# Experts' results computed and stored in quarters of the groups instead of halves, with batch 1's results read last, in a two-layer gated cross-attention kernel

## The reference, cut to what matters

```python
grouped = x.reshape(b, s // g, g, d)                      # g = 32 tokens to a group, 128 groups in all
logits  = jnp.einsum('bntd,des->bntes', grouped, Wc) + bc + tie
perm    = (logits == jnp.max(logits, axis=-3, keepdims=True))   # each of 128 experts picks one token of each group
permuted = jnp.einsum('bntd,bntes->bnesd', grouped, perm)
inner    = relu(jnp.einsum('bnesd,esdf->bnesf', permuted, W1) + b1)     # 512 -> 32 for each expert
result_permuted = jnp.einsum('bnesf,esdf->bnesd', inner, W2) + b2       # 32 -> 512
result   = jnp.einsum('bnesd,bntes->bntd', result_permuted, perm)       # back to the tokens
```

## Time and profile before

| what | us |
|---|---|
| median of 3 runs | 1330.63 (1325.4 to 1336.3) |
| the profiled execution | 1328.46, of which 1326.7 are its span |
| TensorE busy | 1258.9 (95% of the span) |
| VectorE, ScalarE, GpSimd busy | 885.8, 571.2, 554.4 |
| mean granted TensorE clock | 0.984 |

### The profile page before, as it was taken

How to read it: one execution, slowest core, us unless ns; L and a number is a source line. 1 busy time by engine, 2 the same in 40 slices (tenths; PEclk the granted TensorE clock), 3 DMA queues, 4 the chain that set the end, 5 groups by cost and what they waited for, 6 DMA issues and landing times.

```text
span 1326.7 us, 28239 instructions
## 1 busy us (share of the span) xinstructions
PE 1258.9 (95%) x10607; PEld 906.3 (68%) x10607; DVE 885.8 (67%) x1570; ACT 571.2 (43%) x1039; POOL 554.4 (42%) x456
## 2 busy tenths in 40 slices
PE   8999999999999978887989999999998999999998
PEld 7777776777677667621447666766775778888887
DVE  6984787777676546663646766766675977777762
ACT  4345345434542545453562443353336433333331
POOL 3312642454251100000339657856734644444540
PEclk9999999999999979998999999999998999999999
DMA  9765455224411678999983643563323111111101
GB/s 350 225 179 187 154 159 174 101 88 149 141 73 36 208 217 257 321 400 354 400 348 93 222 170 97 174 220 132 121 84 128 64 63 63 63 43 52 63 27 37
DMA packets 126503, 213.59 MB, mean 161 GB/s; under 512 B 27610, under 2 KB 49370, under 8 KB 122332
## 3 DMA queue, kind: packets, MB, share of 16 engines
q1 hardware_dynamic: 126427, 212.57, 47.6%
HBM read 129.92 MB, written 82.62 MB: 160 GB/s over the span
## 4 chain that ended last, share of the span: by engine, by line
PE 77%; DVE 8%; DMA 5%; ACT 4%; issue 3%; SPq 3%; POOL 0%; ACTq 0%; DVEq 0%; POOLq 0%
PE b L157 12%; PE b L158 11%; PE b L159 11%; PE b L1586 5%; PE b L1784 5%; PE b L1785 5%; PE b L1786 5%; PE b L1558 4%; DMA s_rp<-e_chosen 3%; PE b L2080 3%; PE b L1691 3%; PE b L1699 3%; PE b L2098 2%; ACT a_pr L1150 2%; PE b L2114 2%
## 5 line engine op out<-in xcount | busy, mean ns | idle before, releaser
L1150 ACT ACTIVATE a_pr<-b 120x512 f32<-120x512 f32 x252 | 130.2, 603 | 95.1 <-PE b L1586 95.1
L1339 DVE TENSOR_REDUCE a_mx<-b 128x4 f32<-128x480 f32 x256 | 151.9, 651 | 10.4 <-PE b L1558 10.3
L1032 POOL TENSOR_TENSOR a_rp<-a_rp,a_b2s 128x512 f32<-128x512 f32 x96 | 120.5, 1296 | 23.8 <-DMA a_rp<-s_rp 23.8
L1071 POOL TENSOR_TENSOR a_atl<-a_pvs,a_ath 128x512 fp32r<-128x512 f32 x64 | 81.3, 1303 | 81.7 <-ACT a_ath L1194 81.7
L1784 PE MATMUL b<-a_woh,a_ath 128*128 128x512 f32 x256 | 104.6, 409 | 3.1 <-POOL a_atl L1071 3.1
L157 PE MATMUL b<-a_xth,a_wqh 128*128 128x512 f32 x256 | 104.2, 407 | 1.5 <-DVE a_xtl L1314 1.1
L158 PE MATMUL b<-a_xtl,a_wqh 128*128 128x512 f32 x256 | 101.6, 397 | 0.0
L159 PE MATMUL b<-a_xth,a_wql 128*128 128x512 f32 x256 | 101.6, 397 | 0.0
L1786 PE MATMUL b<-a_woh,a_atl 128*128 128x512 f32 x256 | 101.6, 397 | 0.0
L1785 PE MATMUL b<-a_wol,a_ath 128*128 128x512 f32 x256 | 101.5, 397 | 0.0
L1016 POOL TENSOR_TENSOR a_rstd<-a_ve,a_mhalf 128x4 f32<-128x4 f32 x16 | 16.2, 1014 | 190.9 <-DVE a_ve L1261 190.9
(11 more groups left out here) (245 smaller groups left out, 3142.4 us busy)
## 6 DMA issues: line engine op xcount, KB each, us to landing
a_rp<-s_rp SPq DMA_DIRECT2D x128, 256.0 KB, 4.5
s_x<-a_x SPq DMA_DIRECT2D x16, 1024.0 KB, 4.2
s_rp<-e_chosen SPq DMA_DIRECT2D x16, 1024.0 KB, 8.3
s_rp<-e_xc SPq DMA_DIRECT2D x16, 1024.0 KB, 8.4
e_w<-in_w SPq DMA_DIRECT2D x56, 256.0 KB, 4.8
a_xr<-in_x_t SPq DMA_DIRECT2D x8, 1024.0 KB, 6.6
a_x<-in_x SPq DMA_DIRECT2D x8, 1024.0 KB, 10.7
s_xn<-a_xn SPq DMA_DIRECT2D x8, 1024.0 KB, 4.7
```

The source lines that it names most:

```text
L1032: pool.tensor_tensor(rp[:, t, a], rp[:, t, a], b2s[:, :], ALU.add).then_inc(rp_biased, 1)
L1071: pool.tensor_tensor(quarter(atl, q), quarter(pvs, q), f(quarter(ath, q)), ALU.subtract).then_inc(a_lo, 1)
L1150: act.activation(pr[:, h % RING, :], bank[k][0:S2, :], ACT.Exp, scale=SCALE)\
L1339: dve.tensor_reduce(mx[:, t, :, r], bank[k][:, 0:HJ * S2].rearrange("p (a s) -> p a s", a=HJ), AX.X, ALU.max).then_inc(free[k], 1)
```

## The change

- `results(p)` works in quarters: a round is 16 experts (n = 0 to 7), and `round_of(u)` gives quarter 0 for u = 0 to 7, one round after the other, and from u = 8 on quarters 1, 2, 3 of round 0, then of round 1, and so on. Quarter h holds the groups of batches h and h + 4. One p has eight matmuls of 32 rows by 32 columns (two row groups, four column groups) in the place of four of 32 by 64, and fills the same two banks.
- `s_rp` becomes one tensor whose rows are 8,192 + 1,024 numbers long: a store writes 128 runs of 8 KB at a pitch of 36,864 bytes, where it wrote 1 MB in one piece.
- Batch 0's results are read after u = 9 when the first 8 stores have landed. The prologue's marks move forward (`MERGE_AT` 41 to 27, `NORM_AT` 45 to 32, `QUERIES_AT` from 47 to 34, `MAXIMA_AT` from 49 to 36, `ROWS_AT` 58 to 46), the small loads from u = 7 to u = 5.
- Batch 1's results are read after u = 31, when all stores have landed, no longer after u = 22. TensorE's merge tiles of batch 1 move behind scores 2 (tiles 0, 1) and values 1 (tiles 2, 3) in turn 0.
- `s_xn` is laid out chunk, partition, tile, feature: a token load moves rows of 4 KB. Chunk 2's tokens are loaded behind chunk 1's W1 pieces, chunk 3's beside them.
- The hidden activations keep their experts' natural order and have their columns permuted so that each quarter is contiguous.

```diff
-MERGE_AT, WEIGHT_AT, NORM_AT, QUERIES_AT, ROWS_AT = 41, 43, 45, (47, 49, 51, 53), 58
-MAXIMA_AT = {49 + n: (n // 2, (0, 1) if n % 2 == 0 else (2, 3)) for n in range(8)}
+MERGE_AT, WEIGHT_AT, NORM_AT, QUERIES_AT, ROWS_AT = 27, 29, 32, (34, 36, 38, 40), 46
+MAXIMA_AT = {36 + n: (n // 2, (0, 1) if n % 2 == 0 else (2, 3)) for n in range(8)}
...
-        if u == 7:
+        if u == 5:
             load_perm(sp, 0)
...
-        if u == HALF_U:
-            front.half_written(sp)
+        if u == FRONT_U:
+            front.front_written(sp)
             for t in range(NT):
                 load_experts(sp, 0, t)
             load_query_weight(sp)
-        if u == HALF_U + 2:
+        if u == FRONT_U + 2:
...
-        if u == 22:
+        if u == EK - 1:
             for k, uses in TW:
                 sp.wait_ge(full[k], uses.n(None, "merge", 1) + 1)
             load_perm(sp, 1)
+            for q in range(4):
+                front.written(sp, q)
             for t in range(NT):
                 load_experts(sp, 1, t)
...
-    HALF_U = EK // 2
+    FRONT_U = EK // 4 + 1
...
             scores(i, i, 2)
+            if late:
+                merge_tile(i, i + 1, 0)
+                merge_tile(i, i + 1, 1)
             values(1)
...
+            if late:
+                merge_tile(i, i + 1, 2)
+                merge_tile(i, i + 1, 3)
...
+    def round_of(u):
+
+        if u < EK // 4:
+            return 0, u
+        return 1 + (u - EK // 4) % 3, (u - EK // 4) // 3
...
-        return q == 0 or (p >= EK and (p % 2 == 1 or MERGE_AT < p <= NORM_AT))
+        return q == 0 or (p >= MERGE_AT and (p % 2 == 1 or MERGE_AT < p <= NORM_AT))
...
-        sp.dma_start(xc[c % 2][:, q * XQ:(q + 1) * XQ], io["xn"][q * XQ:(q + 1) * XQ].rearrange(
-            "n p d -> p n d")[:, :, c * P:(c + 1) * P]).then_inc(x_in[c % 2][q], 16)
+        tiles = slice(q * XQ, (q + 1) * XQ)
+        sp.dma_start(xc[c % 2][:, tiles], io["xn"][c, :, tiles]).then_inc(x_in[c % 2][q], 16)
...
-            for a in range(EJ):
-                rows, (q, c) = slice(a * EF, (a + 1) * EF), divmod(a, 2)
-                b, _ = result_bank(p, q)
-                ins = pe.matmul(gbank[b][c * NH:(c + 1) * NH, :], inner[rows, k, h * NH:(h + 1) * NH],
-                                w2[k // KS][rows, k % KS, :], start=True, stop=True, skip_group_check=True)
-                if c:
-                    ins.then_inc(g_full[b], 1)
+            for c in range(4):
+                for q in range(2):
+                    a, k = 2 * (p % 2) + q, 4 * n + c
+                    rows, (b, _) = slice(a * EF, (a + 1) * EF), result_bank(p, q)
+                    ins = pe.matmul(gbank[b][c * NQ:(c + 1) * NQ, :], inner[rows, k, h * NQ:(h + 1) * NQ],
+                                    w2[k // KS][rows, k % KS, :], start=True, stop=True, skip_group_check=True)
+                    if c == 3:
+                        ins.then_inc(g_full[b], 1)
...
-    rp_d = [dram(f"s_rp{i}", (EK // 2, P, EJ, D)) for i in range(2)]
+    rp_d = dram("s_rp", (EK // 4, P, 4 * EJ * D + 2 * D))
```

More of the change, by code:

```diff
@@ L1294, in apply @@
             for t in range(NT):
-                dve.tensor_scalar(to[:, t, :], x[:, t, :], mv[:, t, 0:1], rstd[:, t:t + 1],
+                if route:
+                    out, of = to[:, :, t, :], x[:, t, :].rearrange("p (c d) -> p c d", c=C)
+                else:
+                    out, of = to[:, t, :], x[:, t, :]
+                dve.tensor_scalar(out, of, mv[:, t, 0:1], rstd[:, t:t + 1],
                                   ALU.subtract, ALU.mult).then_inc(normed, 1)
@@ L1714, in spread @@
                             ins.then_inc(full[f"s{q}"], 1)
-            if merging:
+            late = merging and first_turn(i)
+            if merging and not late:
                 merge_tile(i, i + 1, 0)
@@ L1844, in experts @@
     RB, RO, KS, RW = 6, 4, 8, 4
-    NH = NG // 2
+    NQ = NG // 4
     EARLY = 2
@@ L1934, in load_ahead @@
             tiles = slice(NTILE - 2 * NT, NTILE - NT)
-            sp.dma_start(xc[0][:, tiles], io["xn"][tiles].rearrange("n p d -> p n d")[:, :, 0:P]).then_inc(x_in[0][3], 16)
+            sp.dma_start(xc[0][:, tiles], io["xn"][0, :, tiles]).then_inc(x_in[0][3], 16)
         else:
@@ L1950, in sync @@
                     load_w1(sp, WG * (c - 1) + s + RW)
+                if c == 1 and s < 4:
+                    load_tokens(sp, 2, s)
+                if c == 1 and s % 2:
+                    load_tokens(sp, 3, s // 2)
                 for n in W2_AT.get((c, s), ()):
@@ L1962, in sync, with front_written @@
                     sp.wait_ge(g_free[b], n + 1)
-            sp.dma_start(io["rp"][2 * u // EK][u % (EK // 2)], slot(u)).then_inc(out_st[u % RO], 16)
+            h, n = round_of(u)
+            sp.dma_start(io["rp"][n, :, h * EJ * D:(h + 1) * EJ * D], slot(u).rearrange("p e d -> p (e d)"))\
+              .then_inc(out_st[u % RO], 16)
             behind[0].load(sp, u)
-    def half_written(sp):
+    def front_written(sp):
         for q in range(RO):
-            sp.wait_ge(out_st[q], 16 * (EK // 2 // RO))
+            sp.wait_ge(out_st[q], 16 * (EK // 4 // RO))
     def written(eng, q):
@@ L2078, in gather @@
                 b, _ = use(SETS * c + s, a)
-                lhs = xc[c % 2][rows, TS * s + t, :] if tokens is None else tokens[rows, t, 0:P]
+                lhs = xc[c % 2][rows, TS * s + t, :] if tokens is None else tokens[rows, 0, t, :]
                 ins = pe.matmul(gbank[b][:, t * ES:(t + 1) * ES], lhs,
@@ L2143, in groups_read @@
     def groups_read(pool, number):
-        b, n = result_bank(EK + number * KS - 1, 1)
+        last = max(u for u in range(EK) if round_of(u)[1] < 2 * number)
+        b, n = result_bank(2 * last + 1, 1)
         pool.wait_ge(g_full[b], n + 1)
@@ L2163, in experts @@
         Begun(load_ahead, gather, emptied, evict_act, evict_dve, on_act, chosen), \
-        Front(cleared, half_written, written, groups_read, spare_banks, banks)
+        Front(cleared, front_written, written, groups_read, spare_banks, banks)
 def feed_forward(nc, tile, sem, eight, ident, mhalf, io):
@@ L2605 @@
     columns = lambda a: a.reshape(C, P).T
-    by_use = lambda a: a.reshape(EK // 2, 2, 2, 2, *a.shape[2:]).transpose(0, 2, 3, 1, *range(4, a.ndim + 2))\
-        .reshape(ES, *a.shape[2:])
+    by_use = lambda a: a.reshape(ES, *a.shape[2:])
     arrays = dict(
```

47 lines of the change are left out of this document (21 added, 26 removed).

## The result

The changed kernel takes 1344.9 us (median of 4 runs, 1342.7 to 1347.8), the kernel before 1331.3 beside it: +13.6 us, ratio 1.0106 with an interval of 1.0080 to 1.0132. The forecast was 1338 and +7.7. The profiled execution took 1347.8 us with a span of 1346.1, which is 19.4 more than the span before; so part of that difference is scatter between executions, and the first thing to find is which part.

What follows compares the result with a forecast made beforehand. TensorE, busy 1258.9 of 1326.7 us, was the bound, with stores' landing pacing the results. Batch 1's later merge, +10.5, less 2.8 coming back gave +7.7: 1330.6 to 1338 us, range 1323 to 1352.

Steps and rivals of the forecast that it cites:

- L: Landing of the last results store: forecast 678 us, before 682.80; prediction wrong if before 670 or after 685.
- Batch 0's reads: Reads of batch 0's results during the results: start at 587 us in the place of 607.32.
- TensorE's restart: TensorE back on results after batch 0's reads: at 610.1 us, 23.1 after they begin, worth 5.7 us.
- The tail: Last results after queries and maxima: store u = 24 issued at 652.8, landed 657.6, then 20.4 us of queue to 678.0.
- Rival 1: Results end early enough: last landing 673, faster reads, full 2.9 back; about 1326 to 1331 us; chance 0.22.
- Batch 1's reads: Reads now behind the last landing: merge tile 3 at 694.8 us, 10.5 later; TensorE stands some 15 us.
- What comes back: Turn 0, merge tile 3 to spread: output weight split during the wait, high parts sooner; 2.8 us back.
- Eight small tiles: Eight matmuls of 32 by 32 per p in the results, for four: nothing gained or lost.
- rival 2: Small tiles in the results go one group after the other: about 1383 us; chance 0.06.
- Tokens: Token loads in 4 KB rows and another order: put at nothing, between -4.8 and +2 us.
- The pitch: Result reads at 1,152 KB pitch: 14.9 us for 16.7, twice, -3.6; left out of the sum, in the range.
- Rival 3: Longer wait after the results: last landing 683, nothing comes back, low clock 3.5 us; 1349 us; chance 0.22.

Runs made afterwards that it cites:

- e6: The kernel before with only batch 1's results read after u = 31 and all landings, merge tiles moved as in the change: 1340.7 us, ratio to before 1.0084.
- e12: The kernel before with each results matmul of 32 by 64 made as two of 32 by 32, over all four row groups: ratio to before 1.0014.
- e4: The changed kernel with three unused matmuls added after each even p from 46 on: ratio to the kernel before 1.0114.
- e1: The changed kernel with the tokens part undone (old layout, 512-byte rows, old load order): ratio to the kernel before 1.0112.
- e3: The changed kernel with quarter 1 for u = 14 to 19 and batch 1's results read after u = 20: ratio to the kernel before 1.0106.
- e2: The changed kernel with each p's two copies shared between ScalarE and VectorE from p = 47 on: ratio to the kernel before 1.0139.

## Why the prediction was right in part

The sign, the place and the chain behind L were right, the range held the time; the size was short by 5.9 us (+7.7 for +13.6). That puts it on the border between the most likely outcome, within 1% (0.62), and slower than that (0.28). By its own signs L at 687.9 would be too late (after 685); counted from the first store, 123.1 us, it is inside that sign's 124.4 (685 - 560.6). Step by step, from the first store on:

- *Batch 0's reads.* Forecast 26.4 us behind the first store (587 - 560.6), measured 26.1.
- *TensorE's restart.* 49.5, measured 49.9 (614.65).
- *The tail.* This is the step that failed. u = 24 was forecast 92.2 behind the first store and came at 94.6: the first 12 us after the restart ran at a clock of 0.56, where I had carried over the rows of before at 1.00, which is the likely cause of these 2.4 us and not shown alone. From there to L I had 25.2 us and it took 28.5: u = 24 landed after 5.6 us and not 4.8, and x, for which I took a store's 2.47, took 4.7. Together 5.7 us, so that L lay 1.0 behind that of before (from the first store) and not 4.7 ahead.
- *Why no gain was left.* Rival 1 priced the reads at the 10.5 us that they take in a full queue, and the sum had L 4.7 us earlier. e6 shows the better way to price them: taken out alone they gave 2.6 us. The part of the queue's time that they gave up became idle, because TensorE was the bound beside them.
- *Batch 1's reads.* Forecast 16.8 us from L to merge tile 3, measured 17.0 (704.89 - 687.9). But TensorE waited on `a_rp` for 4.9 us only and not for 10 to 16. I had it through with the results at about 667.5, 10 us ahead of L; it came to turn 0 at 682.40, 5.5 us ahead, and the turn's own work and waits filled the time until the merge. The half clock isn't what made the wait short: e6, with a clock of 0.96 in the results, came to turn 0 6.7 us ahead of L and waited 4.6. The sum isn't touched by this.
- *What comes back.* Forecast 2.8; from merge tile 3 to the spread it took 13.2 us for 16.5, so 3.3. The high parts came 0.7 us behind the start of the transposes (711.33), as forecast, but not because the output weight was split during the wait for the reads. Its load stands behind them (issued at 698.33), and ScalarE split it while the tokens were being normalised:

```profile
709.50 2.21 ACT L818 ACTIVATE a_woh<-a_raw_o 128x512 fp32r<-128x512 f32 x4
712.02 2.07 ACT L1096 ACTIVATE a_xth<-b 128x512 fp32r<-128x512 f32 x4 [0.31 <-PE b L1522]
```

- *Eight small tiles.* Nothing, shown by e12; rival 2 is out. That the clock would be low beside them I had not seen. In the tail it is hidden behind the queue (e4); in the 2.4 us ahead of u = 24 it probably isn't.
- *Tokens.* Nothing (e1).
- *The pitch.* The reads in the new layout took 10.26 us to issue and the last landed 16.9 us after the first issue (687.91 to 704.84), with the old pitch 16.7. No run shows the 14.9 us that stand in the range and in rival 1.
- *The rivals.* Rival 3 was right on L (its 683 is 122.4 us from the first store, measured 123.1) and on a low clock, wrong in that nothing comes back; its +19 us lies about as far from the measured 13.6 as the forecast does. Rival 1 needed L within 112 us of the first store (673 - 560.6); the shortest here is 119.5. Its break-even at L = 667.5 leaves out the 2.8 us that come back: by the forecast's own sum it is 678 - 7.7 = 670.3. Its -1 and -6 give 1325 to 1330, not 1326 to 1331.

## What to carry to other kernels

A transfer that stands beside a stretch which another engine bounds costs what the stretch gets longer by, not its own length: read the queue's share in that stretch before crediting its removal, or take it out alone and see. Where two resources bound one stretch after the other, moving work between them gains only if they come to overlap; compare kernels by bytes and share over the whole stretch. And cut traces at marks near the change: here two executions of one and the same kernel lay 4.6 us apart at the first mark, as much as the change seemed to cost there.

## What the runs showed of the hardware

- Two kernels with the same 16 small matmuls and the same 2.1 us in a slot (e12 and the changed one) were granted different clocks behind the same kind of results (1.00 and 0.50 from 590 to 600, 0.91 and 0.64 from 590 to 630): in one TensorE is busy for 1.95 of 2.12 us, in the other for 1.60 of 2.10. The kernels differ in more than that, so it is a lead and no proof. Matmuls that nobody needed, put into the gaps of the tail, raised the granted clock there from 0.50 to 0.85 (e4).
- A 1 MB load in rows of 2 KB, between stores that landed every 2.4 to 2.45 us, took 2.65 us in the kernel before, 3.4 in e3, 3.7 and 3.8 in e2 and e4, and 4.7 in the changed kernel. Why it differs stays open.
